# Expert rows gathered inside the step, q turned two maxima later, the last early sum stored first, the last output in three parts

## The reference

```python
xn = layernorm(x)
# branch 1: attention, 16 heads of 32, causal
q, k, v = proj(xn, Wq), proj(xn, Wk), proj(xn, Wv)
q, k = rope(q, k)
attn = softmax(where(causal, q @ k.T / sqrt(32), min))
a = (attn @ v) @ Wo.T
# branch 2: 8 experts, 2 chosen for each token
logits = xn @ gate_w.T                      # (4096, 8)
top_vals, top_idx = top_k(logits, 2)
w = softmax(top_vals)
y_all = einsum('td,eod->teo', xn, expert_w) + expert_b
f = sum(take(y_all, top_idx) * w)
out = x + a + f
```

## Time and profile before

| | |
|---|---|
| runs | 1076.47 us median (1075.51 to 1080.18) |
| profiled execution | 1071.44 us, span 1069.6 us |
| TensorE busy | 935.8 us, 87% |
| VectorE busy | 744.9 us, 70% |
| GpSimd busy | 553.5 us, 52% |
| ScalarE busy | 418.4 us, 39% |
| mean granted clock of TensorE | 0.981 |

### The profile page before, as it was taken

How to read it: one execution, slowest core, us unless ns; L and a number is a source line. 1 busy time by engine, 2 the same in 40 slices (tenths; PEclk the granted TensorE clock), 3 DMA queues, 4 the chain that set the end, 5 groups by cost and what they waited for, 6 DMA issues and landing times.

```text
span 1069.6 us, 18593 instructions
## 1 busy us (share of the span) xinstructions
PE 935.8 (87%) x6525; PEld 447.4 (42%) x6557; DVE 744.9 (70%) x1318; ACT 418.4 (39%) x691; POOL 553.5 (52%) x558
## 2 busy tenths in 40 slices
PE   2898789889998988759999999998888888888887
PEld 1344344444443433425555555543443444434332
DVE  8888889898889798414444444476777766677655
ACT  3367655566554332221222112133343443334432
POOL 1645474665775459163333233175666666666444
PEclk9999999999999999989999999999999999999998
DMA  5456588788773352655555555465544545553333
GB/s 224 126 190 209 147 260 307 194 317 266 256 248 111 110 198 79 256 177 169 170 176 177 178 171 175 131 203 168 169 130 139 169 131 157 157 170 110 90 114 124
DMA packets 107961, 188.61 MB, mean 176 GB/s; under 512 B 11872, under 2 KB 65248, under 8 KB 102624
## 3 DMA queue, kind: packets, MB, share of 16 engines
q1 hardware_dynamic: 97072, 152.03, 42.2%
q0 software_dynamic: 10800, 35.40, 11.6%
HBM read 117.13 MB, written 70.25 MB: 175 GB/s over the span
## 4 chain that ended last, share of the span: by engine, by line
PE 60%; DVE 22%; issue 5%; DMA 4%; POOL 4%; another core or an unknown queue 3%; ACT 2%; SPq 1%; POOLq 0%; DVEq 0%; ACTq 0%
PE psum L923 17%; PE psum L991 7%; PE psum L1015 6%; DVE top L1408 6%; PE psum L1000 6%; PE psum L971 5%; PE psum L958 4%; PE psum L940 4%; PE psum L974 4%; PE psum L900 3%; POOL gT L561 2%; DVE turned_q L1392 2%; DVE rden L1424 2%; DVE den_turned L1422 2%
## 5 line engine op out<-in xcount | busy, mean ns | idle before, releaser
L741 ACT ACTIVATE pT<-psum,factors 128x512 f32<-128x512 f32 (+1 forms) x352 | 221.7, 641 | 350.0 <-PE psum L958 340.8
L1408 DVE TENSOR_REDUCE top<-psum 128x1 f32<-128x384 f32 (+3 forms) x352 | 213.1, 635 | 45.5 <-PE psum L942 35.8
L991 PE MATMUL psum<-xT,w_att 128*128 128x512 f16 x768 | 200.1, 387 | 18.7 <-issue 10.7
L923 PE MATMUL psum<-w_exp,x_gT 128*128 x852 | 196.8, 381 | 6.2 <-DVE x_gT L1364 6.2
L940 PE MATMUL psum<-k_stack,q_stack 96*128 96x384 f16 (+3 forms) x512 | 130.0, 307 | 63.2 <-DVE top L1408 57.5
L596 POOL DMA_INDIRECT x_g<-xn_rows,tok_of x71 | 67.4, 949 | 158.1 <-PE psum L900 136.7
L958 PE MATMUL psum<-q_stack,k_stack 98*128 98x256 f16 (+3 forms) x512 | 129.1, 305 | 7.2 <-ACT pT L741 4.5
L1378 DVE SCALAR_TENSOR_TENSOR y_sb<-psum,down,bias_all 128x512 f32<-128x512 f32 x71 | 53.3, 750 | 104.3 <-PE psum L923 97.9
L923 PEld LDWEIGHTS psum<-w_exp,x_gT 128*128 128x128 f16 x852 | 83.7, 98 | 92.4 <-issue 8.5
L586 POOL TENSOR_TENSOR o_hl<-o_sb,o_hl 128x512 f16<-128x512 f32 x32 | 37.3, 1167 | 164.3 <-ACT o_hl L755 164.3
L765 ACT ACTIVATE x_gT<-psum 128x512 f16<-128x512 f32 x71 | 42.3, 597 | 171.1 <-PE psum L900 171.1
(11 more groups left out here) (158 smaller groups left out, 1256.5 us busy)
## 6 DMA issues: line engine op xcount, KB each, us to landing
y_rows<-y_sb SPq DMA_DIRECT2D x71, 256.0 KB, 2.1
w_in<-w_all SPq DMA_DIRECT2D x12, 1024.0 KB, 9.7
q_stack<-qk_rows SPq DMA_DIRECT2D x96, 128.0 KB
k_stack<-qk_rows SPq DMA_DIRECT2D x96, 128.0 KB
x_in<-x SPq DMA_DIRECT2D x8, 1024.0 KB, 13.6
qk_rows<-q_hl SPq DMA_DIRECT2D x32, 256.0 KB, 2.4
qk_rows<-k_hl SPq DMA_DIRECT2D x32, 256.0 KB
xn_rows<-x_in SPq DMA_DIRECT2D x8, 1024.0 KB, 4.8
```

The costliest lines, as they stand in the source:

```text
L741: act.activation(p_of(j, h, heads), banks[BANK_T + (NT_ * n + k) % 2][:, 0:W], ACT.Exp, scale=factors[:, 0:1]).then_inc(exp_done, 1)
L923: now = pe.matmul(banks[s % 4], x_gT[s % 4][:, xp * C + c, :], w_exp[:, bass.ds(e, 1), wp, c, :].rearrange("p e d -> p (e d)"), start=n == ...
L991: now = pe.matmul(bank, w_att[:, what, wp, c, g * P:(g + 1) * P], xT[b % 2][:, xp * C + c, :], start=at_pass == 0, stop=at_pass == 3 * C - 1)
L1408: return dve.tensor_reduce(out=top[:, h:h + heads, i], in_=banks[BANK_S + k % 2][:, 0:heads * W].rearrange("p (h t) -> p h t", h=heads), a ...
```

## The change

1. Expert rows: late_tiles(n) gives two tiles for every step from 16 on (from step 28 on the second is tile n itself), and GpSimd gathers both within step n, the first after low_qk(0), the second after mask 1. The waits for the last expert tile move from ahead of step 16 into it. late_sb has eight buffers.
2. VectorE turns q after the maxima of units 4 and 5, not before them.
3. In step 15 the early sum is stored ahead of the loads of the experts' matrices.
4. The last group's product with v goes to two pairs of banks, 256 columns each; VectorE divides the first half as one part and the second as two, and writes the high and low halves itself. The last four projections wait for the part they read.

```diff
-        return ([n - G] if n >= N1 else []) + ([n - N1] if N1 <= n < N1 + EARLY else [])
-    LATE = [w for n in range(N) for w in late_tiles(n)] + list(range(N - G, N))
+        return [n - G, n - N1 if n < N1 + EARLY else n] if n >= N1 else []
+    LATE = [w for n in range(N) for w in late_tiles(n)]
-    OUT_LAST = [BANK_QV, BANK_S, BANK_S + 1, BANK_T]
+    OUT_LAST = [BANK_QV, BANK_S, BANK_S + 1, BANK_O]
+    HALF_LAST = [(BANK_O, BANK_DEN), (BANK_T, BANK_T + 1)]
...
 @@ sync, step 15
+                    for w in out_tiles(n - 1):
+                        store_early(w)
                     sp.wait_ge(tok_summed, 1)
                     for e in range(4, E):
                         load_exp(e)
                     sp.wait_ge(wo_done, EARLY)
                     load_exp(0)
...
 @@ gpsimd, step(n)
                 mask(n, 0)
-                if n + 1 == N:
-                    gather_y(N - 3)
                 if n + 3 < N:
                     low_qk(0, n + 3)
+                if n == N1:
+                    pool.wait_ge(y_done, NTILE)
+                    for u in range(4):
+                        pool.wait_ge(y_stored[u], 16 * len(range(u, NTILE, 4)))
+                for w in late_tiles(n)[:1]:
+                    gather_y(w)
                 if n + 3 < N:
                     rope(1, n + 3)
                 mask(n, 1)
+                for w in late_tiles(n)[1:]:
+                    gather_y(w)
...
             for n in range(N1, N):
                 step(n)
-                for w in late_tiles(n + 1) if n + 1 < N else ():
-                    gather_y(w)
-                if n + 2 == N:
-                    gather_y(N - 4)
-            gather_y(N - 2)
-            gather_y(N - 1)
-            low_o(N - 1)
...
 @@ tensor
+            def times_v_last(i, first, last):
+                q0, q1 = i * J // 2, (i + 1) * J // 2
+                o, den = (banks[k] for k in HALF_LAST[i])
+                b, g = (N - 1) // G, (N - 1) % G
+                for j in range(first, last):
+                    pe.wait_ge(masked, J * (N - 1) + j + 1)
+                    q = max(q0, j)
+                    for h in range(HG):
+                        pe.matmul(o[h * HD:(h + 1) * HD, q * P:q1 * P], ...)
+                    for h in range(HG):
+                        now = pe.matmul(den[h * HD:(h + 1) * HD, q * P:q1 * P], ...)
+                if last == q1:
+                    now.then_inc(pv_done, 1)
...
-            times_v(N - 1, 2)
-            times_v(N - 1, 3)
-            pe.wait_ge(exp_done, NT_ * N - 1)
+            pe.wait_ge(exp_done, NT_ * N)
+            times_v_last(1, 0, 2)
+            pe.wait_ge(o_last, 1)
             project_out(N - 1, OUT_LAST[J - 1], 0, 9)
-            pe.wait_ge(o_lo, N)
+            times_v_last(1, 2, 4)
             for j in range(J):
+                pe.wait_ge(o_last, max(j, 1))
                 project_out(N - G + j, OUT_LAST[j], 9, 12)
...
 @@ vector
+            def normalise_last(first, last):
+                i = first // (J // 2)
+                o, den = (banks[k] for k in HALF_LAST[i])
+                t = slice(first * P, last * P)
+                few = slice(first * P // HD, last * P // HD)
+                hl = o_hl[(N - 1) // G % 2]
+                dve.wait_ge(pv_done, J * (N - 1) + i + 1)
+                own.link(dve.transpose(den_turned[:, t], den[:, t]))
+                own.link(dve.reciprocal(rden_few[:, few], ...))
+                own.link(dve.transpose(rden[:, t], ...))
+                if first == 0:
+                    dve.wait_ge(o_lo, N - 1)
+                dve.tensor_tensor(o_sb[:, t], o[:, t], rden[:, t], ALU.mult)
+                own.link(dve.tensor_tensor(hl[:, G - 1, 0, t], o[:, t], rden[:, t], ALU.mult))
+                dve.tensor_tensor(hl[:, G - 1, 1, t], o_sb[:, t], hl[:, G - 1, 0, t], ALU.subtract).then_inc(o_last, 1)
...
 @@ vector, step(n)
+                if nxt:
+                    largest_score(n + 1, 4)
+                    largest_score(n + 1, 5)
                 if ahead:
                     rotate(0, n + 3)
-                if nxt:
-                    largest_score(n + 1, 4)
-                    largest_score(n + 1, 5)
...
-            add_experts(N - 4)
-            add_experts(N - 3)
+            normalise_last(0, 2)
             add_attention(N - 5, BANK_KO)
-            normalise_o(N - 1)
-            add_experts(N - 2)
-            add_experts(N - 1)
+            normalise_last(2, 3)
+            normalise_last(3, 4)
             for j in range(J):
                 add_attention(N - G + j, OUT_LAST[j])
```

More of the change, by code:

```diff
@@ L189, in moe_attention_layer @@
     idx_y = [at(f"idx_y{u}", [P, 2], I32) for u in range(4)]
-    late_sb = [at(f"late_sb{u}", [P, D], F32) for u in range(6)]
+    late_sb = [at(f"late_sb{u}", [P, D], F32) for u in range(NLATE)]
     assert place[0] <= slot[8]
@@ L482, in _ @@
                     load_exp(0)
-                for w in out_tiles(n - 1):
-                    store_early(w)
+                if n != CHOOSE + 4:
+                    for w in out_tiles(n - 1):
+                        store_early(w)
                 for w in out_tiles(n):
@@ L514, in _ @@
                     store_late(n - 5)
-                    for w in late_tiles(n - 1)[1:]:
-                        store_late(w)
+                    if n - 1 < N1 + EARLY:
+                        store_late(n - 1 - N1)
                 if n + 1 < N:
                     for w in late_tiles(n + 1):
-                        load_late(w)
-                if n + 2 >= N:
-                    for w in ([N - 4], [N - 3, N - 2, N - 1])[n + 2 - N]:
                         load_late(w)
@@ L532, in _ @@
                     stack(1, n + 3)
-            store_late(N - 5)
-            for w in late_tiles(N - 1)[1:]:
+            for w in range(N - 5, N):
                 store_late(w)
[L536 to L539, removed]
+            for u in range(NLATE):
+                sp.wait_ge(out_stored[u], 16 * len(range(u, NT, NLATE)))
         @block.gpsimd
@@ L976, in times_v @@
                 now.then_inc(pv_done, 1)
+            def times_v_last(i, first, last):
[6 more added lines that the diff above has]
+                    for h in range(HG):
+                        pe.matmul(o[h * HD:(h + 1) * HD, q * P:q1 * P], v_sb[b % 2][:, j, g * P + h * HD:g * P + (h + 1) * HD],
+                                  p_of(j, h, 1)[:, (q - j) * P:(q1 - j) * P], start=j == 0, stop=j == q1 - 1)
+                    for h in range(HG):
+                        now = pe.matmul(den[h * HD:(h + 1) * HD, q * P:q1 * P], ones32[:], p_of(j, h, 1)[:, (q - j) * P:(q1 - j) * P],
+                                        start=j == 0, stop=j == q1 - 1)
+                if last == q1:
+                    now.then_inc(pv_done, 1)
             PASSES = ((0, 0), (0, 1), (1, 0))
@@ L1114, in step @@
                     project_v(n + G, BANK_QV, 3, 6)
-                times_v(n, 0)
+                if nxt:
+                    times_v(n, 0)
+                else:
+                    pe.wait_ge(v_read, J * B)
+                    pe.wait_ge(o_read, N - 1)
+                    times_v_last(0, 0, 1)
                 shifted_scores(n, 7)
@@ L1136, in step @@
                 shifted_scores(n, 10)
-                times_v(n, 1)
+                if nxt:
+                    times_v(n, 1)
+                else:
+                    times_v_last(0, 1, 2)
                 if wo:
@@ L1479, in step @@
                     read_logits(KEEP_AT[n])
-                if ahead:
-                    rotate(0, n + 3)
                 if nxt:
@@ L1484, in step @@
                     largest_score(n + 1, 5)
+                if ahead:
+                    rotate(0, n + 3)
                 if n == 0:
```

28 lines of the change are left out of this document (13 added, 15 removed).

## The result

The changed kernel takes 1117.92 us median of 4 runs (1117.11 to 1118.51) against 1075.99 (1072.22 to 1080.18) of the kernel before: ratio 1.040, 95% interval 1.037 to 1.044, 4% slower. The profiled execution took 1118.02 us, its span is 1116.3 and the mean granted clock 0.956. Steps 16 to 27 alone grew from 285.3 to 336.4 us, and the clock of that stretch fell from 0.99 to 0.92.

What follows compares the result with a forecast made beforehand. It saw TensorE waiting for VectorE's maxima before, and a gather loop through four engines bounding late steps after. 55 - 9 - 11.3 = +34.7 on 1071.4 gives 1106, plus 5.0 to the median: 1111, range 1086 to 1140.

Steps and rivals of the forecast that it cites:

- The loop through the gathers: Late steps: gathers inside the step close a loop through four engines, 26.0 us, 27.7 with half clock, against 23.95 before.
- Half clock: Late steps: TensorE work between the hole before its third block of scores and the division runs slower, 1.7 us a step.
- The landing by the page's formula: Gathers in late steps: an estimated landing of 2.6 us instead of 3.56 makes the loop 1.0 shorter, time about 1096.
- The late signals: VectorE's division in late steps: its late start, 1.7 us a step, goes since no gather is then in flight.
- A sign that failed: Steps 17 to 28: VectorE's add waits some 3 to 5 us for the second tile's rows, less for the first's.
- q turned later: Steps 0 to 14: turning q two maxima later shortens TensorE's wait for maxima, -9 us, between 0 and -14.
- The store: Step 15: storing the last early sum first removes TensorE's 10.29 us hole and half clock behind it, -11.3 us.
- The end: From group 30's division to the last add: taken as 0 us change, ends -1.3 and +2.5.
- no half clock: Rival, chance 0.2: late-step loop of 26.0 us, sum +11.7, time 1088.
- the old median of the landing: Rival, chance 0.2: gathers land in 5.9 us, 2.3 more in 15 steps, +35, time 1146.
- the signals staying: Rival, chance 0.08: late signals before the division remain, 1.7 us in 15 steps, +26, time 1137.
- The side that was to be faster: Rival, chance 0.07: second tile there by 18.9 us after the first maximum, TensorE the bound at 21.1, time 1024.

Runs made afterwards that it cites:

- Gathers a step ahead: Changed kernel with gathers at the same two places of GpSimd's step, but for the next step's tiles: 1034.90 us, ratio 0.9865 to the kernel before.
- filled hole: Changed kernel with 16 extra products, whose result nothing reads, ahead of TensorE's third block of scores in steps 17 to 30: 1103.88 us, ratio 1.0496.
- q turned first: Changed kernel with q turned ahead of the maxima of units 4 and 5, as in the kernel before: 1123.25 us, ratio 1.0451.
- groups 2 and 3: Two of three groups of follow-up runs, each on one chip; the kernel before took 1074.99 us in group 2 and 1076.23 in group 3.
- group 1: One of three groups of follow-up runs, each on one chip; the kernel before took 1050.31 us in it.

## Why the prediction was right

It said 1111 and the time is 1117.9. The medians differ by 41.9 us, the two profiled executions by 46.6, since that of the kernel before was 4.5 below its median. The forecast added 5.0 us for that gap, and the changed kernel's profiled execution has none; by the stages the forecast was 12 us short, and 5 of these were made good by luck. Stage by stage, in the two profiled executions:

| | predicted | measured |
|---|---|---|
| steps 0 to 14 | -9 | -6.2 |
| step 15 and the experts | -11.3 | -10.6 |
| steps 16 to 27 | +42.5 | +51.1 |
| steps 28 and 29 | +11.1 | +11.3 |
| step 30 to group 30's division | +1.4 | -0.4 |
| from there to the last add | 0 | +1.5 |
| sum | +34.7 | +46.7 |

- *The loop through the gathers* holds. The second tile's last gather was to be issued at 20.15 us plus 1.7 for the clock, 21.85; in the step shown it is at 22.25, on average of steps 17 to 27 at 22.5. The landing was put at 3.56; in nine of these steps the add begins 3.5 to 3.7 us after that issue, and in the two others it waits for the first tile's add. Gathers a step ahead remove the loss, so the cause is tested and not only fitting.
- *Half clock* was the term with no direct row, 1.7 us a step; the filled hole measures 1.3. The 4.45 us hole is what "some 3.9 in one piece" named, and it stands where it was to stand.
- *The landing by the page's formula*: the Trainium skill (DMA: Bandwidth & Descriptors, Anatomy of one DMA) gives an estimate of 2.6 us for 256 KB, 1.0 less a step. No landing that the trace of the changed kernel has took under 3.3, so the measurement decides against it.
- *Where the 8.6 us of steps 16 to 27 were missed*: the eleven steps from 17 on took 28.3, not 27.7 (6.7). By the averages the working is right, or up to 0.3 us too long, as far as the second mask. Then the second tile's copy and first gather take 2.5 us instead of 1.77: the copy took 0.64 where VectorE's add of the first tile had begun before it (nine of eleven steps) and 0.18 where it hadn't (two), and the gather behind it mostly 1.36 instead of 1.02. The working priced both from a place where no add runs beside them. Step 16 took 24.9, not 23.1 (1.8). Half clock isn't the reason there: its 4.42 us hole stands at its end, and the granted clock of its first 6 us is 1.00. VectorE waits 0.67 and 0.81 us for TensorE's scores in it before q's turn, and the copy and the gather are long as well.
- *low_o* (1.16 us on GpSimd behind VectorE's division and ScalarE's high half) was left out of the loop. It doesn't lengthen it, since q's turn takes as long beside it, but it makes the sentence "the gathers start 1.07 later, which now counts" wrong: turning q later cost the loop next to nothing, as q turned first showed.
- *The late signals* went from the late steps, as the loop assumed: in steps 16 to 29 no gather is issued within 5 us of the end of the products. The reason given, a gather in flight, is not what the runs show; it is a gather being issued, and not on every chip.
- *A sign that failed*: the first tile's wait for its rows was to be the lesser. It is 5.6 us on average in steps 17 to 27 and the second's is 4.0 (none in two of them, where the first tile's rows come only 6.5 us after their last issue).
- *q turned later* is worth 6 us in the early steps in this pair of traces and 9 in the kernel before with q later only. Over all traces the first maximum of step 15 comes at 425 to 432 us with q later (nine) and at 435 to 440 with q first (five). *The store* was right in place and size.
- *The end* is 1.5 long instead of 0, inside its bounds. The products of the first half end at 1095.57 and its division starts at 1100.07: behind the last gathered tiles' adds it comes 4.5 us late, more than the 1.5 us that the division in parts gives where the gathers are a step ahead.

The rivals: no half clock (26.0) comes near the filled kernel's 26.9, not this one; the old median of the landing (5.9) and the signals staying did not show. The side that was to be faster needed the second tile by 18.9 us; it came at 25.9.

## What to carry to other kernels

Moving a gather nearer to its use turns a transfer that ran beside the work into a link of a loop: add up the loop through all engines, instruction by instruction, and price each instruction for what will run beside it (here a copy of 0.18 us that takes 0.64 beside VectorE's add). Test an edit of several parts by its parts: two of the four (q later, store first) are worth 1.9% (1.5 to 2.3) and 1.0% (0.8 to 1.3) alone, and with the gathers left at the end of the step ahead the same change is 2.5 to 3.4% faster than the kernel before. A pause of GpSimd between gathers at the moment at which another engine is signalled can pay for itself where the late start below shows; measure it on more than one chip.

## What was not expected of the hardware

In the first pair of traces and in groups 2 and 3, VectorE's start on TensorE's signal is late when the products end while GpSimd is issuing a gather: by 1.5 to 1.8 us in most late steps of the kernel before, and 0.8 to 1.1 us after that gather has ended; where more gathers follow it is up to 3.1 us late. Three copies of 0.2 us that move the gather away gave back 1.7% of the kernel. In group 1 there is none of it in four traces, though 19 divisions lie alike. One place is the same in every kernel: in step 15 the products end 0.82 us into a gather of x_g, and the division starts 0.07 us later in the four traces of group 1 and 2.0 to 2.1 us later in the ten others.

What sets the groups apart isn't known: each is one chip at one time. Whether it is the signal or VectorE that is held stays open too. The kernel before most likely takes 1050 us instead of 1075 in group 1 for this reason: its own trace has 14 such late starts, 25.5 us in all (an estimate; it was not traced in group 1). The version with the gathers at the end of the step and the gap added was not tried.
